# Two bias rows added by TensorE through the identity instead of by GpSimd, in a hybrid scan, expert and attention kernel

## The reference, cut to what matters

```python
x = x + mamba(layernorm(x))       # a scan with 32 states per feature, out_w, out_b, own residual and norm
x = x + ffn(layernorm(x))         # 8 experts of 256 x 256, the best 2 of 8 per token
x = x + block_b(layernorm(x))     # linear causal attention, then an MLP of 1024, with a residual inside
x = x + ffn(layernorm(x))         # the same experts again
```

## Time and profile before

| what | value |
|---|---|
| median of 3 runs | 1843.38 us (1839.24 to 1846.09) |
| the profiled execution's own time | 1845.13 us |
| its span | 1843.3 us |
| granted TensorE clock over the span | 0.94 |
| TensorE matmul instructions | 16992 |
| VectorE instructions | 5957 |
| ScalarE busy | 926.0 us |

### The profile page before, as it was taken

The page is one execution under the profiler, slowest core; times in us unless marked ns, Lnnn a source line. Parts: engine busy times, 40 slices in busy tenths (PEclk is TensorE's granted clock), DMA queues, the critical chain, the costliest instruction groups (busy, mean ns, idle before and its releaser), DMA issues. The chain is left out here.

```text
span 1843.3 us, 55933 instructions
## 1 busy us (share of the span) xinstructions
PE 1693.8 (92%) x16992; PEld 1422.4 (77%) x16992; DVE 1565.0 (85%) x5957; ACT 926.0 (50%) x2134; POOL 245.1 (13%) x515
## 2 busy tenths in 40 slices
PE   5774889999999999999999999999999999999987
PEld 3332668787887878787888878787878878787986
DVE  6589879899998989898999999898989999997522
ACT  4674445463645555554645555455536455554322
POOL 1011011111102011110102020111101020111000
PEclk9886879999999989998999999899989999999998
DMA  6885333242333333332433323332423333330000
GB/s 191 298 247 147 110 94 99 77 117 75 102 96 90 100 84 110 91 96 77 110 87 93 107 81 98 100 99 81 117 71 93 105 89 104 93 98 20 1 7 6
DMA packets 108425, 182.63 MB, mean 99 GB/s; under 512 B 45288, under 2 KB 71936, under 8 KB 107648
## 3 DMA queue, kind: packets, MB, share of 16 engines
q1 hardware_dynamic: 107232, 178.71, 33.9%
q10 hardware_dynamic: 928, 0.56, 0.1%
HBM read 161.35 MB, written 17.83 MB: 97 GB/s over the span
## 5 line engine op out<-in xcount | busy, mean ns | idle before, releaser
L1635 DVE CUSTOM_DVE_ANT_0 state<-decayed_state,u_ring 128x128 f32<-128x128 f32 x2048 | 522.3, 293 | 11.1 <-ACT u_ring L928 4.7
L1626 DVE TENSOR_TENSOR decayed_state<-state,decay 128x128 f32<-128x128 f32 x2048 | 508.1, 289 | 2.7 <-POOL m_rstd L813 1.2
L1300 PE MATMUL bank<-f_w_sb,hs_whole 128*128 128x256 f32 x2048 | 488.3, 382 | 0.6 <-DVE res L1748 0.6
L928 ACT ACTIVATE u_ring<-xrep,b_steps 128x256 f32<-128x256 f32 x1024 | 450.5, 503 | 52.5 <-DVE state L1635 46.0
L1300 PEld LDWEIGHTS bank<-f_w_sb,hs_whole 128*128 128x128 f32 x2048 | 374.2, 191 | 45.9 <-DVE res L1748 1.0
L1035 ACT ACTIVATE hs_whole<-bank,f_b_sb 128x256 f32<-128x256 f32 x512 | 214.1, 470 | 373.1 <-PE bank L1287 373.1
L1287 PE MATMUL bank<-late_fT_parts,f_w_hi 128*128 128x256 f32 x1024 | 187.6, 306 | 0.0
L1287 PE MATMUL bank<-fT_parts,f_w_hi 128*128 128x256 f32 x1024 | 179.5, 297 | 4.6 <-DVE fT_parts L1678 3.4
L1220 PE MATMUL bank<-state,cblk 128*32 128x256 f32 x2048 | 151.3, 423 | 16.4 <-DVE state L1635 16.4
L1287 PEld LDWEIGHTS bank<-fT_parts,f_w_hi 128*128 128x128 f32 x1024 | 142.5, 189 | 23.3 <-DVE fT_parts L1678 7.1
L1287 PEld LDWEIGHTS bank<-late_fT_parts,f_w_hi 128*128 128x128 f32 x1024 | 149.8, 194 | 11.8 <-issue 5.8
(11 more groups left out here) (157 smaller groups left out, 2296.3 us busy)
## 6 DMA issues: line engine op xcount, KB each, us to landing
xrep<-xs_dram SPq DMA_DIRECT2D x1024, 128.0 KB, 2.6
xt<-in_x SPq DMA_DIRECT2D x4, 1024.0 KB, 7.7
xn_dram<-xn SPq DMA_DIRECT2D x4, 1024.0 KB, 5.6
xs_dram<-xs SPq DMA_DIRECT2D x8, 512.0 KB, 4.4
f_w_sb<-in_f_w SPq DMA_DIRECT2D x2, 2048.0 KB
z_dram<-zT SPq DMA_DIRECT2D x8, 512.0 KB, 4.5
z_t<-z_dram SPq DMA_DIRECT2D x64, 64.0 KB, 2.3
out<-x SPq DMA_DIRECT2D x64, 64.0 KB, 2.1
```

Source lines behind the costliest of these rows:

```text
L928: act.activation(u_ring[:, s % USLOTS], xrep[:, slot, n], ACT.Copy, scale=b_steps[:, s // BSTEPS, s % BSTEPS:s % BSTEPS + 1]).then_inc(u_m ...
L1300: last = pe.matmul(bank_[:, tile * D:(tile + 1) * D], hs_whole[:, slot, m, tile * P:(tile + 1) * P], w(m), start=(m == 0 and tile == 0 and ...
L1626: dve.tensor_tensor(decayed_state[:, part], state[:, (s - 1) % RING, part], decay[:, part], ALU.mult).then_inc(decayed.sem, 1)
L1635: dve._custom_dve(add_sat, out=state[:, s % RING, part], in0=decayed_state[:, part], in1=u_ring[:, s % USLOTS, part], s0=LIMIT, s1=-LIMIT) ...
```

## The change

It takes GpSimd's additions of `out_b` (`add_to_normed`) and of `mlp_b2` (`add_mlp_bias`) away. `add_attention` now adds `res` and `a_t` directly into `mb`, with the waits of both earlier additions. A new function `add_row` issues one matmul of 512 columns: the stationary operand is the 128 x 128 identity, the moving operand is a bias row, which every partition holds, repeated for both tiles, and it accumulates into a bank that already has its sum. It is issued once after the eight matmuls of `mamba`, into `OB[0]`, and once after the last `mlp_second`, into `OB[1]`. The semaphores `mamba_out` and `mlp_made` are now set by these. In `mamba` only the first matmul of the bank starts a sum, where before the first one of each tile did. L1771 waits for the tokens' DMAs instead of for GpSimd's addition, and for the whole `mb_done` of the late chunk, which is now one increment.

```diff
-        xnb_done = signal("xnb_done", 1)
-        mb_done = signal("mb_done", 2)
+        mb_done = signal("mb_done", 1)
...
-                def add_to_normed():
-                    pool.wait_ge(tok_in.sem, tok_in.after(c, 16 * 3 * B))
-                    pool.wait_ge(y_tposed.sem, y_tposed.after(c, 1))
-                    pool.tensor_tensor(xn_t[:], xn_t[:], both("out_b"), ALU.add).then_inc(xnb_done.sem, 1)
...
-                def add_mlp_bias():
                     if late is not None:
                         pool.wait_ge(x3_done.sem, x3_done.after(late, 1))
-                    pool.wait_ge(acc_done[0].sem, acc_done[0].after(c, TILES * E))
-                    pool.tensor_tensor(mb[:], res[:], both("mlp_b2"), ALU.add).then_inc(mb_done.sem, 1)
...
                 def add_attention():
                     pool.wait_ge(xr_done.sem, xr_done.after(c, 1))
-                    pool.wait_ge(mb_done.sem, mb_done.after(c, 1))
-                    pool.tensor_tensor(mb[:], mb[:], a_t[:], ALU.add).then_inc(mb_done.sem, 1)
+                    pool.wait_ge(acc_done[0].sem, acc_done[0].after(c, TILES * E))
+                    if late is not None:
+                        pool.wait_ge(x3_done.sem, x3_done.after(late, 1))
+                    pool.tensor_tensor(mb[:], res[:], a_t[:], ALU.add).then_inc(mb_done.sem, 1)
...
-                add_to_normed()
                 add_to_tokens()
...
                 rstd_of(c, OUTER)
-                add_mlp_bias()
                 next_cblk(3)
...
+            def add_row(bank_, row):
+                return pe.matmul(bank_[:], ident[:], rows[row][:].unsqueeze(1).broadcast_to([P, TILES, D]),
+                                 start=False, stop=True, skip_group_check=True)
...
-                    last = second_products(OB[1], j % 2, lambda m: g["m_w2"][:, 2 * j + m, :], more=j > 0, ends=j == 3)
+                    last = second_products(OB[1], j % 2, lambda m: g["m_w2"][:, 2 * j + m, :], more=j > 0, ends=False)
                     if j == 3:
-                        last.then_inc(mlp_made.sem, 1)
+                        add_row(OB[1], "mlp_b2").then_inc(mlp_made.sem, 1)
...
-                                             start=(k == 0), stop=(k == KD - 1))
-                    last.then_inc(mamba_out.sem, 1)
+                                             start=(k == 0 and tile == 0), stop=False, skip_group_check=True)
+                    add_row(OB[0], "out_b").then_inc(mamba_out.sem, 1)
...
                     dve.wait_ge(mamba_out.sem, mamba_out.after(c, 1))
-                    dve.wait_ge(xnb_done.sem, xnb_done.after(c, 1))
+                    dve.wait_ge(tok_in.sem, tok_in.after(c, 16 * 3 * B))
...
                     dve.wait_ge(mlp_made.sem, mlp_made.after(late, 1))
-                    dve.wait_ge(mb_done.sem, mb_done.after(late, 2))
+                    dve.wait_ge(mb_done.sem, mb_done.after(late, 1))
```

More of the change, by code:

```diff
@@ L851, in next_cblk @@
                     set_cblk(i + (u + PARTS - 1) // UNITS, (u + PARTS - 1) % UNITS)
-                def add_to_normed():
-                    if c is None:
-                        return
-                    pool.wait_ge(tok_in.sem, tok_in.after(c, 16 * 3 * B))
-                    pool.wait_ge(y_tposed.sem, y_tposed.after(c, 1))
-                    pool.tensor_tensor(xn_t[:], xn_t[:], both("out_b"), ALU.add).then_inc(xnb_done.sem, 1)
                 def add_to_tokens():
```

## The result

The changed kernel takes 1891.48 us (median of 4 runs, 1886.32 to 1893.36) against 1843.72 us before (4 runs, 1839.24 to 1846.09): a ratio of 1.0258, with a 95% interval of 1.0229 to 1.0286. The forecast was 1846.2 us with a range to 1857. It was wrong by 45 us, and no rival reached the result either.

The account below looks back on a forecast made before the run. TensorE was taken as pace-maker over most of a step, VectorE leading at its start. Terms of +1.5, +0.86 and +0.43 us sum to +2.8, on 1843.38 us giving 1846.2 us; range 1838 to 1857.

Parts of the forecast that it names:

- The clock falls more or less often.: Rival: steps change between short and long with the granted clock; two steps worth 9 us, 1837 or 1855 us; chance 0.08.
- the 1.5 us for the 14 steps: Steady loop: each step 0.11 us longer by VectorE's 0.10 or TensorE's 0.07 us and the restart, +1.5 us in all.
- The added rows, each alone.: Each added 128x512 f32 matmul takes 0.43 us of TensorE, with ends of 0.25 and 0.86 us.
- Row one, inside a steady step: Row after `mamba`: 0.43 us over a cover of 0.34 us, so L1771 and its chain start about 0.10 us later.
- Both rows on TensorE's own queue.: At the transposes and the next stop, idles of 0.79 us cover 0.86 us of rows, leaving 0.07 us a step.
- The slower rival with rows of 0.86 us each: Rows on the path: 1.7 us a step less 0.79, plus 2.6 for the ends, gives 1859 us; chance 0.03.
- The ends of the program: Step without a scan +0.86 us, last step's `add_mlp` +0.43 us, first step nothing.
- What GpSimd loses.: Removed additions L858 and L872: L1669 returns 11.8 us of VectorE, absorbed by the query product's wait; taken as zero.
- The waits that move: L1771's token wait, `add_attention` as one addition and L1771's wait for the late chunk's addition: each zero.

Follow-up runs that it names:

- the 68: 68 empty TensorE instructions per step ahead of the scores, four in each of 17 blocks: changed kernel 1839.40 us, kernel before 1828.25 us (repeat 1830.40).
- the late 16: Changed kernel with 16 empty TensorE instructions per step directly ahead of the scores' waits, behind the scan's output products: 1860.73 us, ratio 1.0056.

## Why the prediction was wrong

**The sum by the runs.** Without gaps the change costs 11.2 us, measured on one chip. The price of a gap is read in the profiled runs. Before, the four steps with one take 104.67 us on average and the other ten 100.84: 3.8 us. After, the thirteen take 105.28 us, and a step of the same kernel with the 68 takes 101.49: 3.8 us again. Nine more gaps at 3.8 us are 34.5 us; with the 11.2 that makes 45.7, against 47.8 measured, and the gap in the first chunk is not in it yet. So about three quarters are the gaps and one quarter the rows.

**"The clock falls more or less often."** This step failed most. I saw that a long step has a clock of 0.95 and made the clock the cause, with "nothing says on which side a step then falls". The trace of before had it: the waits list 9.3 us of issue in four places at L1408, and the four stand in the four long steps. Had I opened one long and one short step side by side, as I opened one at its start, I would have had a gap at a fixed count of pairs, and so a cause that counts instructions. The rival was also priced at two steps, at 9 us, where nine more changed kind; the 1.5 us for the 14 steps held nothing for it at all.

**"The added rows, each alone."** The 0.43 us is right for a record, but a call of `add_row` gives two: `mamba` has four calls in the code and eight records in the earlier trace rows, which I counted as eight matmuls. The row starts two loads 0.43 us apart, 0.86 us a row and 1.7 us a step. By this the trace agrees with the Trainium skill's FP8 and Floating Point Precision, section TensorE Precision Notes, whose four passes I had set aside: a call of 512 columns takes 0.86 us, and my estimate from the four passes had been 0.85.

**"Row one, inside a steady step"** had the right mechanism and a wrong size. Its timeline after:

```profile
1104.80 1.99 PE L1350 MATMUL bank<-out_w_sb,z_t 128*128 128x256 f32 x8
...
1106.63 1.02 PE L1210 MATMUL bank<-out_b_sb,ident_sb 128*128 128x512 f32 x2
...
1107.69 0.69 DVE L1759 TENSOR_TENSOR res<-bank,xn_t 128x512 f32<-128x512 f32 x1 [0.45 <-PE bank L1210]
```

I had 0.43 of row less 0.34 of cover, 0.10 us; it is 0.86 less 0.34, about 0.5, and VectorE's idle shows 0.45. In all chunks:

```profile
DVE res L1759 <- PE bank L1210: 9.6, 16, 3.0
```

**"Both rows on TensorE's own queue."** The two idles were cover, as said. The timeline at the transposes, against the earlier trace rows:

```profile
1118.11 0.60 PE L1222 MATMUL bank<-ident_sb,turn 128*128 128x128 f32 x4
...
1119.24 0.59 ACT L976 ACTIVATE turn<-bank 128x512 f32<-128x512 f32 x1
...
1119.87 0.69 DVE L1666 TENSOR_TENSOR fT_parts<-turn,fT_parts 128x512 fp32r<-128x512 f32 x1 [0.42 <-ACT turn L976]
```

The transposes wait for nothing but TensorE's queue, and the forecast's "L1678 is not held further" became a wait of VectorE for ScalarE's copy (12.8 us in 15 places after, 6.3 us in one place before). With 1.72 us of rows less 0.79 of cover, the forecast's own method gives 0.93 us a step, where 0.88 was found (101.23 against 100.35 in the short steps of the runs without gaps, over the 101 us that the prediction had named as its sign of being wrong). The agreement is in part luck: for the output projection's row alone the method gives 0.86 - 0.34 = 0.5 us and for the MLP's alone 0.86 - 0.79 = 0.07, where 0.78 and 0.2 were found. The slower rival with rows of 0.86 us each, 1859 us, had therefore about the right size for this part, 13 to 16 us for 11.2. I gave it 0.03.

**"The ends of the program"** had the right places and the same half size: from the last gating to the end the rows cost 2.4 us in the runs with the 68 (152.64 against 150.28), where 1.29 was forecast and twice that is 2.6.

**"What GpSimd loses."** L1669 fell from a median of 810 ns to 408, as said, and the wait behind it grew: the query feature waits 34.8 us for the product instead of 25.4. The runs with the 68 show that this is L872's addition: 35.0 us without rows and 34.0 with the MLP's row, but 25.2 where only the output projection's addition is gone. Most of the 11.8 us stopped there. I took zero; 1.5 to 5 us is what the runs leave.

**"The waits that move"** held: GpSimd's single addition and the tokens' wait delay nobody.

**What stays open.** Why a block asked for behind TensorE's wait comes too late in most steps when its place is directly behind it (44) and only in some when it is eight further on (36), and what differs between two steps that are alike up to the scores. In the changed kernel the step without a gap and the next one, with a gap, agree on all engines within 5 ns over the 40 us ahead of the scores, and yet the packet starts 1.5 us ahead of them in one and 1.8 us behind in the other. The DMA queues were empty in the window above, so it was not held up by other transfers there. That the place behind the wait decides was shown by one kernel (the late 16) against another with the same boundary; that the wait itself does it, and not the full queue of products behind it, was not tried apart.

## What to carry to other kernels

Idle time by "issue" at a fixed count inside a run of many small matmuls was a shortage of instructions here; look for it in the waits, and count, before you give the length of a step to the clock. An edit of a few instructions anywhere in a loop moves all block boundaries behind it, so compare two versions only with the gaps out of both, or you read their place and not the edit: here 8 empty instructions were worth +24 us in the kernel before (1875.48 against 1851.97) and -49 us in the changed one (1842.12 against 1891.48, on another chip). Count records of the trace, not calls of the source, when a new call is to be priced.

## What the runs showed of the hardware

- TensorE's instructions come in blocks of 16.4 KB while the program runs (146 packets), 250 to 270 instructions each by the counts above. 128 pairs of 64 columns take 1.4 us, so one block is used up in about that time. In the loop, with the boundary behind the 106th or 110th pair, the engine did not stop where the next block's packet started 0.9 us or more ahead of the run of pairs; where it started 0.9 us or more into the run, the engine stood for 1.9 to 2.8 us and went on 2.2 to 3.2 us after the packet's start.
- Inside the loop the boundaries are counted from the loop's start, not from the program's (number 1302 behind the branch in 61 of 64 gaps), and every pass takes nine packets again.
- Two executions of one program may differ in how many steps stall: the kernel before spreads over 1830 to 1863 us in these runs, and over 1827 to 1832 us with 16 or 68 empty instructions per step.
- An empty instruction among long products costs nothing that was measured: 1842.12 us with 8, and 1841.24 and 1839.40 with 40 and 80 per step (34 and 68 of them ahead of the scores).
- A gap of 1.9 to 2.8 us costs 3.8 us a step; the granted clock falls behind it (0.58 over 4 us, 0.50 for three of them). The shorter gaps of the late 16 cost 1.6 us each (1440.2 against 1420.7 us for the 14 steps, 12 gaps).
